# Gathering a token's second row with addition onto its first row, instead of adding the two on VectorE

## The reference

```python
gate_logits = jnp.einsum('bsd,de->bse', x, gate_w) + gate_b
weights, indices = jax.lax.top_k(gate_logits, TOP_K)          # TOP_K = 2 of 8 experts
weights = jax.nn.softmax(weights, axis=-1)
h = jnp.einsum('bsd,edh->ebsh', x, w1) + b1[:, None, None, :]
xh, gh = jnp.split(h, 2, axis=-1)
out_e = jnp.einsum('ebsf,efd->ebsd', jax.nn.silu(gh) * xh, w2) + b2[:, None, None, :]
sel = jnp.take_along_axis(out_e, indices[..., None], axis=2)
ffn = jnp.sum(sel * weights[..., None], axis=2)
x = _layernorm(x + ffn, axis=-1)                              # no scale, no bias
```

## Time and profile before

| | us |
|---|---|
| median of the three runs | 1410.84 |
| the execution that was profiled, as timed | 1414.7 |
| its span in the profile | 1412.7 |
| TensorE busy in the span | 1273.8 (90%) |
| VectorE busy | 1141.0 (81%) |
| ScalarE busy | 797.1 (56%) |
| GpSimd busy | 782.9 (55%) |

### The profile page before, as it was taken

How to read it: one execution, slowest core, us unless ns; L and a number is a source line. 1 busy time by engine, 2 the same in 40 slices (tenths; PEclk the granted TensorE clock), 3 DMA queues, 4 the chain that set the end, 5 groups by cost and what they waited for, 6 DMA issues and landing times. The chain is left out here.

```text
span 1412.7 us, 40515 instructions
## 1 busy us (share of the span) xinstructions
PE 1273.8 (90%) x13336; PEld 1052.4 (74%) x13337; DVE 1141.0 (81%) x2631; ACT 797.1 (56%) x1862; POOL 782.9 (55%) x743
## 2 busy tenths in 40 slices
PE   4789999999999999899988899999999999999990
PEld 2456666666666676667677899899999999999990
DVE  4789999999999999899977987768576858685666
ACT  5566666667666766676635344444444444444446
POOL 3367677677766787687775433416061707070771
PEclk9799999999999999999967999999999999999996
DMA  6123322334443223321234331312203120301444
GB/s 216 37 73 121 116 96 88 119 119 134 135 135 99 95 66 124 109 86 57 91 114 150 107 122 30 106 50 74 74 30 119 55 95 30 126 28 33 135 138 157
DMA packets 82097, 137.33 MB, mean 97 GB/s; under 512 B 9120, under 2 KB 64928, under 8 KB 81888
## 3 DMA queue, kind: packets, MB, share of 16 engines
q1 hardware_dynamic: 70880, 92.83, 20.5%
q0 software_dynamic: 10848, 42.32, 9.4%
q10 hardware_dynamic: 288, 1.19, 0.2%
HBM read 98.83 MB, written 37.47 MB: 96 GB/s over the span
## 5 line engine op out<-in xcount | busy, mean ns | idle before, releaser
L1098 PE MATMUL pe<-arena 128*128 128x128 f16 x3408 | 219.5, 221 | 19.9 <-issue 19.9
L1098 PEld LDWEIGHTS pe<-arena 128*128 128x128 f16 x3408 | 203.3, 98 | 25.4 <-issue 24.7
L1098 PE MATMUL pa<-arena 128*128 128x128 f16 x3408 | 218.5, 220 | 0.0
L1555 ACT ACTIVATE arena<-pe,arena 128x128 f32<-128x128 f32 x568 | 161.6, 370 | 75.9 <-PE pe L1098 75.4
L1098 PEld LDWEIGHTS pa<-arena 128*128 128x128 f16 x3408 | 201.1, 98 | 0.0
L1123 PE MATMUL py<-arena 128*128 (+1 forms) x1704 | 197.6, 273 | 1.0 <-DVE arena L2345 1.0
L1688 DVE SCALAR_TENSOR_TENSOR arena<-pa,arena 128x511 f32<-128x511 f32 (+2 forms) x240 | 178.7, 745 | 14.3 <-ACT arena L1196 8.2
L1123 PEld LDWEIGHTS py<-arena 128*128 128x128 f16 x1704 | 163.5, 98 | 19.0 <-issue 1.3
L1727 DVE TENSOR_TENSOR_SCAN arena<-arena,pe 128x512 f32<-128x512 f32 x128 | 148.7, 1203 | 3.2 <-issue 1.8
L2539 POOL TENSOR_SCALAR arena<-arena 128x1536 f16<-128x1536 f32 (+2 forms) x35 | 43.7, 1248 | 185.9 <-DVE arena L2345 180.8
L2297 DVE SCALAR_TENSOR_TENSOR pm<-pa,arena 128x128 f32<-128x128 f32 x284 | 80.5, 351 | 77.7 <-ACT arena L1555 73.9
(11 more groups left out here) (308 smaller groups left out, 2584.9 us busy)
## 6 DMA issues: line engine op xcount, KB each, us to landing
arena<-step_rows SPq DMA_DIRECT2D x64, 512.0 KB, 5.7
arena<-in_w_exp POOLq DMA_DIRECT2D x32, 768.0 KB, 4.8
arena<-queue SPq DMA_DIRECT2D x74, 129.5 KB
answer<-arena SPq DMA_DIRECT2D x71, 128.0 KB
arena<-in_x SPq DMA_DIRECT2D x16, 512.0 KB, 6.5
answer<-zeros SPq DMA_DIRECT2D x10, 512.0 KB, 4.8
arena<-h SPq DMA_DIRECT2D x9, 512.0 KB, 6.1
h<-arena SPq DMA_DIRECT2D x8, 512.0 KB, 3.0
```

The costliest lines, as they stand in the source:

```text
L1098: ins = pe.matmul(bank[:, f * P:(f + 1) * P], w_split[:, p, hl, d * 2 * FF + col:d * 2 * FF + col + P], x[:, r, d, :], start=(n == 0), sto ...
L1555: ins = e.activation(sg[:, half, f, :], GATE[half][:, f * P:(f + 1) * P], ACT.Silu, bias=b1a[:, bass.ds(ex_, 1), ff], scale=1.0 / S1)
```

## The change

The high rows no longer go to `high`. The indirect DMA that gathers them is issued with an addition, so that each landing row is added to the row that is already in `total`. Since the low rows must be there by then, GpSimd waits for `low_got` (all 32 low gathers) before it issues the first of the 32 adding gathers. VectorE loses the five TENSOR_TENSOR of `spread_of` and its wait for `low_got`, and its twelve SCALAR_TENSOR_TENSOR with a running sum become twelve TENSOR_REDUCE of a row. `high` stays as the place where ScalarE's squares go.

```diff
@@ -2412,11 +2412,7 @@
             def spread_of(b):
-                if b == 0:
-                    dve.wait_ge(low_got, 16 * NTILE)
                 dve.wait_ge(got[b], 16 * LG)
-                rows_b = total[:, b * LG:(b + 1) * LG, :]
-                fin_step(dve.tensor_tensor(rows_b, rows_b, high[:, b * LG:(b + 1) * LG, :], ALU.add))
                 for k in range(LG):
                     ins = dve.bn_stats(fst[:, b, k], total[:, b * LG + k])
                 fin_step(ins)
@@ -2430,8 +2426,7 @@
                 dve.wait_ge(got[b], 16 * LG)
                 for k in range(LG):
                     row = total[:, b * LG + k]
-                    ins = dve.scalar_tensor_tensor(row, row, 1.0, high[:, b * LG + k], ALU.mult, ALU.add,
-                                                   accum_out=row_sum[:, b, k:k + 1])
+                    ins = dve.tensor_reduce(row_sum[:, b, k:k + 1], row, AX.X, ALU.add)
                 fin_step(ins)
@@ -2832,6 +2827,11 @@
+            def add_rows(dst, t, which, done):
+                pool.indirect_dma_start(dst[:, t, :], None, answer,
+                                        bass.IndirectOffsetOnAxis(ap=slot_lh[:, which, t:t + 1], axis=0),
+                                        compute_op=ALU.add).then_inc(done, 16)
+
@@ -2843,11 +2843,12 @@
             for t in range(NTILE):
                 get_rows(total, t, 0, low_got)
             pool.wait_ge(need_ready, 1)
+            pool.wait_ge(low_got, 16 * NTILE)
             for b in range(NB):
                 for s in range(WB):
                     wait_tiles(s, pool.value_load(need_i[0:1, b * WB + s:b * WB + s + 1], min_val=1, max_val=NJ // WB))
                 for k in range(LG):
-                    get_rows(high, b * LG + k, 1, got[b])
+                    add_rows(total, b * LG + k, 1, got[b])
```

## The result

The changed kernel takes 1416.7 us (median of seven runs, 1414.32 to 1419.82); the kernel before, run beside it, 1411.34 (seven runs, 1409.07 to 1412.86). The ratio is 1.0042, with a 95% interval from 1.0026 to 1.0057: slower by 0.4%, clear of no change. The forecast was 1408.6 and a small gain. The time lies inside the stated range, 1407 to 1426, but on the other side of the kernel before, on that of the first rival.

A forecast was written before the change was run, and what follows sets the result against it. The tail was taken as bound by VectorE, then ScalarE; 2.2 us off for two additions less ScalarE's lateness, 0 for everything else under cover, took 1410.84 to 1408.6 us, range 1407 to 1426.

The forecast's parts named there:

- the first rival: GpSimd's adding gathers: its part of one twice as long, distance 2.20 us, group 7 17.5 us late, 1426.1 us; chance 0.29.
- What bounds the tail: Behind the last tile: about 10 us with VectorE's work on the path, then about 18 with ScalarE's.
- The saving: In the tail: two of five additions on the path, less ScalarE's lateness of 0.3 us, gain 2.2 us.
- the reductions: VectorE's twelve row totals: TENSOR_REDUCE at 409 ns against 422 fused, taken as no change; at most 0.3 us for four.
- the sum: Group 7 lands at 1349.7 + 31 g + 3.0, against its need at 1403.4; in all -2.2 and 0 us.
- The new wait: GpSimd before the first adding gather: 3.0 us landing, 2.8 for three numbers; start at 1349.7, 4.6 late, under cover.
- When each group is needed: VectorE at `got[b]`: group 0 needed at 1380.86, group 3 about 1387.3, group 6 about 1398.8, group 7 at 1403.4.
- The limit of 1.63 us: Largest distance between starts of adding gathers on GpSimd at which the change costs nothing; group 7 decides.
- The distance g: Time between starts of adding gathers on GpSimd: no row shows it, taken as 1.25 to 1.58 us.
- the rivals over it: GpSimd's adding gathers too slow (1426.1 us, chance 0.29), or two reads costing GpSimd too (distance 1.72, 1411.2 us, chance 0.10).
- Landing: Adding gathers' time from issue to landing: 3.0 us, from plain gathers' 2.7 to 4.4.
- DMA engines: Gathers' queue: 0.45 us of each engine per gather, doubled 0.90, under 1.25; engines 85% busy with the others' 13%.

The follow-up runs named there:

- dve_saving_alone: The changed kernel with plain gathers into the second tile and no GpSimd wait for the first rows, second rows left out of the output: 1409.66 us, ratio 0.9987.
- low_wait_alone: The kernel before with only GpSimd's wait for all first rows added ahead of the second rows' gathers, which stay plain: 1413.91 us, ratio 1.0008.
- plain_but_spaced: The changed kernel with plain gathers into the second tile, each followed by a GpSimd MEMSET, second rows left out of the output: 1428.25 us, ratio 1.0097.
- half_size_gathers: The changed kernel with gathers of 64 rows of 1 KB (groups 0 to 3) or 128 rows of 512 B (4 to 7); run once, for instruction prices only.

## Why the prediction was wrong

- **What bounds the tail: right.** Two parts, VectorE until the squares of group 3 and ScalarE behind them, and only the first two additions on the path. The saving was put at 2.2 us; it measured 2.4 (dve_saving_alone). TENSOR_REDUCE took 409 ns, as in the earlier trace rows, but the reductions were put at nothing and gave 0.10 us: four of them with the next instruction's start are 1.42 us against 1.52 for the fused form with its read-outs. The other 0.1 is that ScalarE began its squares 0.19 us after the start of the roots before them, where the sum had 0.28.
- **The new wait: right.** The first adding gather was put 5.8 us behind the last low one (3.0 to land, 2.8 for three numbers); it measured 5.76, and low_wait_alone showed it to be free under the slack. The price of a number was SyncE's, not GpSimd's; that it fitted is partly luck.
- **When each group is needed: right.** Group 7 is needed 22.9 us after the last L2345 begins, and the last group decides. plain_but_spaced met the sum within 0.4 us at a distance that nobody had planned. The limit of 1.63 us came near by two errors that nearly cancel: with the 4.56 us that the last adding gather took to land, and a first one that started 31.8 us ahead of the last L2345 and not 30.8, it is 1.62.
- **The distance g: wrong, and it decides the sign.** The step that failed is "What g is no row shows", where the plain gather's time was split into an index list (0.3) and rows (0.65), and the rows' part alone was let grow by half: 1.25 to 1.58, all under the limit. Measured: 1.85. The split was itself the fault. It came from comparing a gather with direct DMAs, which tells nothing of how a gather's time goes with rows, and half_size_gathers shows that the greater part goes with neither rows nor bytes. So scaling "the rows' part" bounded nothing. Nor had the half a row behind it: the same part doubled gives 1.90, over the limit. The same text had 2.20 as the other end and held it for the range, with the limit in between at 1.63, nearer to the low end. A value spread evenly from 1.25 to 2.20 would lie over the limit with a chance of 0.6; the rivals over it had 0.39.
- **Landing: mis-sized.** 3.0 us was taken from the plain gathers; adding ones took 4.2, the last 4.56. That added 1.6 us to the lateness of group 7.
- **The sum with the right terms.** With g = 1.85 and 4.56 to land, in the times of the profile before: 1349.7 + 57.3 + 4.6 = 1411.6, 8.2 us after 1403.4. Less the 2.2 us saved, which the 1403.4 has in it, that is 6.0 slower. The gathers began 1.0 us sooner against the last tile than assumed (31.8 us ahead of the last L2345, not 30.8), which leaves 5.0, and the tail measured 5.0.
- **DMA engines: right.** From 1346 to 1377 us the gathers' queue of the changed kernel took 47.9%, 14.8 us of each engine, for 2.07 MB, the bytes of 15.8 gathers of 128 KB: 0.94 us each, where a plain one takes 0.45 (the prediction's doubled figure was 0.90). Over all 32 adding gathers, 1346 to 1409 us at 47.6%, it is 0.94 too. It didn't decide the distance, as 0.94 is still far under 1.85. The Trainium skill, in "Collectives: The Full Stack", in the section on the bandwidth ceiling, gives half the rate of a copy for the adding step of a ReduceScatter, because it reads two sources. The doubled engine time of this trace agrees with that; no run here shows the reason.
- **The first rival: right in kind.** Its place (group 7 at `got`) and its mechanism hold, and its point of no gain, 1.70, would be 1.69 with the measured terms; groups 5 and 6 were late as well. Its size was too large: it doubled GpSimd's part, 0.95 us, which measured 1.54, 1.6 times as long. So the time came out at 1416.7 and not at its 1426.1.

## What to carry to other kernels

Moving an addition from an engine into a DMA pays only where that addition is on the path, so count first which ones are (here two of five), and move only those: 8 adding gathers kept the 2.4 us that 32 turned into a loss of 5.0. A queue with slack hides a delay entirely until the distance per item times the number of items behind it uses the slack up, so the number to know is the break-even distance, and an operation without a row should be priced by one measured instruction before it is used 32 times. And look first for idle time just ahead of the path: VectorE's 3.09 us of waiting for the last tile took the same two additions for 0.1 us.

## What the runs showed of the hardware

- An adding gather of 128 rows occupies GpSimd for 1.54 us against 0.95 for a plain one (after, before); at 64 rows it is 1.41 against 0.89, and the width of the row, 1 KB or 512 B, makes no difference (half_size_gathers).
- It lands 4.2 us after its issue (3.7 to 5.6) against 3.0 (2.7 to 4.4), and makes 96 packets more (3072 over 32 gathers). Its packets take 0.94 us of each DMA engine against 0.45.
- GpSimd's reading of three numbers is hidden between plain gathers, but after a wait it stands in the open: 2.9 us between the landing of the last low row and the first adding gather, and 3.19 behind the MEMSET between two groups in plain_but_spaced.
